# One core, a feed-forward, attention, feed-forward chain: the order of the routing work in the first two blocks

## The reference

```
x = x + 0.5 * ffn(layernorm(x))
x = x + attention(layernorm(x))
x = x + 0.5 * ffn(layernorm(x))

ffn(h):   z = w_norm * h * rsqrt(mean(h*h) + 1e-6)
          probs = softmax(z @ w_router)                      # 32 experts
          w, sel = top_k(probs, 4)
          each expert takes its tokens in order of arrival, 128 at most:
              y_e = (silu(z_e @ w_gate[e]) * (z_e @ w_up[e])) @ w_down[e]    # width 176
          out = sum of w * y_e over the chosen experts
          shared = sigmoid(z @ w_shared_gate) * (silu(z @ sw_gate) * (z @ sw_up)) @ sw_down   # width 704
          return h + out + shared
attention: 16 query heads, 8 key and value heads of width 32, rotary positions,
           scores capped by 50 * tanh(s / 50), causal softmax, output projection
```

## Time and profile before

| | before |
|---|---|
| median of 3 runs | 939.04 us |
| profiled execution | 939.21 us, its span 937.5 us |
| TensorE busy | 910.2 us (97% of the span) |
| VectorE busy | 696.1 us (74%) |
| ScalarE busy | 531.8 us (57%) |
| GpSimd busy | 511.3 us (55%) |
| mean granted TensorE clock | 0.999 |

### The profile page before, as it was taken

One profiled execution on the slowest core, in us unless ns is written; L12 is line 12 of the kernel. 1 busy time (PEld: TensorE's weight loads), 2 busy tenths in 40 slices (PEclk: granted clock), 3 DMA queues, 4 the chain that ended last, 5 costly groups with the idle time before them and its releaser, 6 DMA issues.

```text
span 937.5 us, 18000 instructions
## 1 busy us (share of the span) xinstructions
PE 910.2 (97%) x6118; PEld 685.5 (73%) x6118; DVE 696.1 (74%) x1704; ACT 531.8 (57%) x794; POOL 511.3 (55%) x537
## 2 busy tenths in 40 slices
PE   7999999999999999999999999989999999999997
PEld 6878887777778856666666666558788877777786
DVE  6998787554444889989998999988887875544435
ACT  6666743132233478878887888876667431322322
POOL 6343305555652588887888788934432045655530
PEclk9999999999999999999999999999999999999999
DMA  8143228777774510010001002004432187777725
GB/s 260 49 137 107 74 86 214 178 178 182 181 191 92 179 46 24 23 42 26 23 23 45 22 12 79 24 12 131 142 99 73 56 232 173 183 178 183 173 38 178
DMA packets 95512, 101.89 MB, mean 109 GB/s; under 512 B 18768, under 2 KB 86736, under 8 KB 95440
## 3 DMA queue, kind: packets, MB, share of 16 engines
q1 hardware_dynamic: 83152, 83.17, 28.7%
q0 software_dynamic: 12288, 17.83, 11.2%
HBM read 65.44 MB, written 35.54 MB: 108 GB/s over the span
## 4 chain that ended last, share of the span: by engine, by line
PE 67%; DVE 18%; issue 6%; ACT 5%; POOL 3%; DMA 0%; DVEq 0%; POOLq 0%; SPq 0%; ACTq 0%
PE zT L1048 8%; PE gu L1068 7%; PE gu L90 7%; PE gu L92 6%; PE gu L91 6%; PE pj_at L90 3%; PE down L90 3%; PE down L92 3%; PE down L91 3%; PE pv_at L1766 3%; PE pj_at L92 3%; PE pj_at L91 3%; PE zT L1057 2%; PE scores_at L1750 2%; DVE turned_at L2008 2%
## 5 line engine op out<-in xcount | busy, mean ns | idle before, releaser
L90 PE MATMUL gu<-x_hi,gu_hi 128*128 128x512 f32 x264 | 120.7, 457 | 0.8 <-DVE act_gu L1351 0.7
L820 POOL DMA_INDIRECT rows<-z_rows,slots x64 | 69.0, 1078 | 67.7 <-DVE slots L1342 49.1
L1868 ACT ACTIVATE capped_at<-scores_at 128x2048 f32<-128x2048 f32 x64 | 93.1, 1455 | 20.5 <-PE scores_at L1750 20.2
L92 PE MATMUL gu<-x_lo,gu_hi 128*128 128x512 f32 x264 | 103.9, 394 | 0.0
L91 PE MATMUL gu<-x_hi,gu_lo 128*128 128x512 f32 x264 | 103.6, 392 | 0.0
L1128 ACT CAST a_hi<-act_gu 128x512 fp32r<-128x512 f32 x96 | 59.2, 617 | 75.9 <-DVE act_gu L1351 63.1
L1876 ACT ACTIVATE probs_at<-capped_at 128x2048 f32<-128x2048 f32 x64 | 95.1, 1486 | 2.5
L90 PE MATMUL down<-down_hi,a_hi 128*128 128x256 f32 x300 | 93.9, 313 | 0.6 <-DVE a_lo L1361 0.4
L1230 ACT ACTIVATE y<-gu,rows 128x256 f32<-128x256 f32 x64 | 30.3, 474 | 109.7 <-PE gu L1068 94.6
L1945 POOL TENSOR_SCALAR_AFFINE_SELECT probs_at<-probs_at 128x1024 f32<-128x1024 f32 x64 | 85.6, 1342 | 9.6 <-ACT probs_at L1876 8.9
L1048 PE MATMUL zT<-w_gu,xT 128*128 128x352 f32 x256 | 86.3, 460 | 0.0
(11 more groups left out here) (262 smaller groups left out, 2602.5 us busy)
## 6 DMA issues: line engine op xcount, KB each, us to landing
w_gu<-in_w_gate SPq DMA_DIRECT2D x64, 176.0 KB, 2.6
w_gu<-in_w_up SPq DMA_DIRECT2D x64, 176.0 KB, 3.2
w_down<-in_w_down SPq DMA_DIRECT2D x64, 176.0 KB
z_rows<-z SPq DMA_DIRECT2D x16, 512.0 KB, 3.8
acc<-base SPq DMA_DIRECT2D x10, 512.0 KB, 3.2
out<-base SPq DMA_DIRECT2D x10, 512.0 KB, 3.2
xn_at<-acc SPq DMA_DIRECT2D x16, 256.0 KB, 2.7
x<-xn_at SPq DMA_DIRECT2D x16, 256.0 KB, 2.1
```

The source lines that it names most:

```text
L90: nc.tensor.matmul(out, w_hi, x_hi, start=first, stop=False)
L92: return nc.tensor.matmul(out, w_hi, x_lo, start=False, stop=last)
L820: pool.indirect_dma_start(out=gathered_rows[:, n, :], out_offset=None, in_=m.z_rows, in_offset=bass.IndirectOffsetOnAxis(ap=slots[:, e:e + ...
L1868: nc.scalar.activation(capped[:, u % 2, :, 0:n], scores[:, :, 0:n], ACT.Tanh, scale=QK_SCALE / SOFTCAP).then_inc(capped_ready, 1)
```

## The change

TensorE, for block 0 in `slot`: `router(2)` now stands ahead of `count(1)`, not behind it. For other blocks and in the second stage nothing changes there.

VectorE, block 0 (`first_slot`): `statistics(3)` is written out as its two parts, and `take_counts(1)` stands between them; before, it stood behind `outputs(0, 0)`.

VectorE, block 1 of the first stage (`slot`): `product(1, 3)` stands ahead of `top_experts(3)`, and `weigh(2)` behind `top_experts(3)`; before, `weigh(2)` stood ahead of `a_lo_part(1, 0)` and the product behind the ranking. No instruction is added or taken away.

```diff
@@ on_tensor, slot @@
                 down_block(b)
+                if s is not None:
+                    router(s)
                 if b == 0:
                     count(r)
-                if s is not None:
-                    router(s)
@@ on_vector, first_slot @@
                 weigh(f)
                 top_experts(r)
-                statistics(s + 1)
+                for j in range(TJ):
+                    read = front.read(dve, s + 1, j)
+                take_counts(r)
+                front.variances(dve, s + 1, read)
                 outputs(0, 0)
-                take_counts(r)
                 weigh(r)
                 outputs(0, 1)
@@ on_vector, slot @@
                 product(b, 1)
-                if b == 1 and not before:
+                behind_head = b == 1 and not before
+                if behind_head:
                     statistics(s)
-                weigh(f)
+                else:
+                    weigh(f)
                 a_lo_part(b, 0)
                 a_lo_part(b, 1)
                 product(b, 2)
+                if behind_head:
+                    product(b, 3)
                 top_experts(r)
-                product(b, 3)
+                if behind_head:
+                    weigh(f)
+                else:
+                    product(b, 3)
                 a_lo_part(b, 2)
```

## The result

In 19 runs of each kernel, taken in alternation, the changed kernel has a median of 941.05 us (939.67 to 945.30) against 939.13 (939.01 to 939.55). The ratio on record is 1.0018, with a 95% interval of 1.0012 to 1.0025; the two medians alone give 1.0020. The time lies inside the forecast range of 938.2 to 941.4. Whether the loss is under or over 0.2% is not decided: the ratio is just under it, the interval reaches to both sides, and 941.05 is over the 940.9 us at which the prediction drew that line.

A forecast was written before the change was run, and what follows sets the result against it. TensorE, busy nearly all the time, was taken as the bound. Router and counts -0.05, block 1 to +0.9, handed on to +1.3 us: 939.04 becomes 940.3 us; range for eight in ten 938.2 to 941.4.

The forecast's parts named there:

- Router and counts: Blocks 0 and 1: TensorE's stands of 1.02 and 0.52 us go, but are spent waiting for z(3); worth -0.05 us.
- The copy within the statistics: VectorE, block 0: the counts' copy delays the aggregation of block 3's statistics by 0.05 us, bounds 0 and 0.13.
- Block 1: VectorE stands 2 us before product(1,3); late low parts make TensorE's down projection wait; +0.9 us at its sixth part.
- The gain at chunk 10: TensorE, block 1: the 0.69 us stand ahead of chunk 10 goes, so count(3) comes that much earlier.
- Handed on: Into block 2: z(5) on ScalarE delays the copy of block 4's logits, so TensorE's lateness becomes +1.3 us.
- +1.3: The forecast's total lateness in us, reached at the logits of block 4 and taken as kept to the end.
- rival (d): Block 1, between chunks 1 and 2: the new stand and eight spaced transposes cost clock, 1.6 us; 941.9 us, chance 0.07.
- one stretch of 3.1 us: Evidence against a clock loss: from 9.21 to 12.35 only eight spaced transposes ran, and the next matmul was not slower.
- (c): VectorE's full 1.97 us is handed on through low parts, outputs and block 4's router; 941.0 to 941.2 us, chance 0.12.
- (a): Block 1: low parts are early enough after all, only the 0.69 us gain stays; 938.4 us, chance 0.12.
- (b): All three TensorE stands vanish and z(3) does not hold turn(3); 936.8 us, chance 0.05.

The follow-up runs named there:

- e3: The third edit alone (product(1,3) ahead of top_experts(3), weigh(2) behind it) against the kernel before: median 939.87 us, ratio 1.0005.
- e1: The first two edits alone (router(2) ahead of count(1), counts within the statistics) against the kernel before: median 940.63 us, ratio interval 0.9985 to 1.0021.
- e2: The first edit alone (router(2) ahead of count(1)) against the kernel before: three runs at 939.06 to 939.23 us, seven at 939.62 to 940.29, two at 942.55 and 942.79.
- e5: The changed kernel again, nothing altered, to profile a longer execution; against the kernel before: ratio 1.0025, profiled execution 946.22 us.
- e4: The changed kernel with six additional unused matmuls of 512 columns ahead of turn(3): eleven runs at 939.59 to 940.36 us, one at 945.92.

## Why the prediction held, and where not

**Router and counts.** As forecast: both stands vanish, z(3) holds `turn(3)` at the same time. The copy within the statistics, taken at 0.05 us from bounds of 0 and 0.13, cost 0.00. e3 against the changed kernel confirms that the two edits give TensorE nothing.

**Block 1.** The mechanism was right in each step; some sizes were off. VectorE's stand was 1.90 us (forecast 2). The ranking took 66.00 - 62.77 = 3.23 us and not 3.46, the length read from the earlier trace rows; the difference is in its last instruction, `chosen`, 0.93 us there and 0.69 here. So product(1,4) came at 67.97 and not at 68.22, and the low parts some 0.2 earlier than forecast: the stands ended at 69.31 and 70.09, where 69.5 and 70.3 were forecast. That is why the sixth part moved by 0.62 and not by 0.9.

The gain at chunk 10 was mis-sized too, 0.92 at count(3) where 0.69 was forecast. An idle time in a row counts from the modelled end of the last matmul (0.39 us long), while the next can start 0.23 behind its start, 0.16 before that end; so 0.69 of idle time are 0.85 us of delay, and 0.05 is the offset of the two traces. It changed nothing behind it, since TensorE then stood for the low parts: from 67.18 to 72.31 the first ten groups took 5.13 us against 3.59, 1.54 more (forecast 1.5), although the idle times in the rows, 0.81 and 0.15, add up to 0.96. The logits of block 4 moved by 0.97, not 1.3.

**Handed on.** The sum stopped at those logits. I had seen that VectorE follows with less lateness, and did not price it. In the kernel before, the router of block 5 waited for its low parts; when TensorE is late, that wait is covered. The kernel before, then the changed kernel:

```profile
85.04 0.50 PE L90 MATMUL zT<-x_hi,router_hi 128*128 128x512 f32 x1 [0.16 <-DVE x_lo L677]
```

```profile
85.69 0.51 PE L90 MATMUL zT<-x_hi,router_hi 128*128 128x512 f32 x1
```

The counts of block 4 are 0.97 late (85.45 against 84.48), the next logits 0.64 (90.03 against 89.39), and that stays: the six short runs have a median of 939.72, 0.59 over that of before. The term "+1.3" was mis-sized; it is +0.6, half of the difference lost at the logits of block 4 and half at this router.

**Clock, rival (d).** This is where the judgement failed: the sum put the clock at nothing. The rival had 0.07; by the times and clocks of the runs it happened in 12 of 19, and its price of 1.6 us came out (1.5 between the groups, 1.6 in e1's trace). I had set against it one stretch of 3.1 us at the start of one execution, in which the clock held. What holds in one execution need not hold in the next: the changed kernel does both. And the length of 3.1 us was no bound, since in e2 2.0 us were enough. That the price fits is in part luck. It was taken from the slower transposes at the start of the run, read as a low clock, but the clock rows of the kernel before read 1.00 there (columns as at e1), so that reading is not shown:

```profile
3.60:5.00 1.40, 1.32 (x6) 1.32 (x7) 1.36 (x4) 0.00 (x0) 0.54 (x3) 1.00 0.46 64
8.00:9.30 1.30, 1.21 (x12) 0.97 (x9) 1.07 (x4) 0.28 (x1) 1.14 (x6) 1.00 1.03 412
```

The rule of the Trainium skill, page "TensorE: Matmul & The Clock Gate", section "HAM oscillation — how this bites in real kernels", that pauses between bursts put the array back to its low clock, agrees with e1, e2 and e5, where the clock row reads 0.57 to 0.67 behind the stand. The waits in that section's example are longer than the stand of e2; here the measurement decides. e4 shows the cause: with the stand filled the long group is gone. That the eight transposes have a part in it is not shown; e2 does without them. What decides between the two outcomes in one and the same kernel stays open.

The median of 941.05 lies 0.75 over the forecast, the sum of a constant part forecast 0.7 too large and a clock part left out of it. That it fell inside the range is luck in part. The range held it because it reached over (c), which didn't happen, and because two errors of opposite sign met: with the forecast's +1.3, a long run would be at (d)'s 941.9, outside. The median also depends on how many runs lose the clock, which nobody had priced. The chance for slower by over 0.2% was, by what the runs show, too small: twelve of the 19 runs are 0.16 to 0.30% longer than the median of before, and one 0.66%.

**Rivals (a), (b), (c)** are excluded for the changed kernel by its trace: TensorE stood for low parts, z(3) held, and VectorE's 1.7 us was not handed on whole.

## What to carry to other kernels

Pulling work forward on the busiest engine gathered its waits in front of the next fixed date and won nothing here; before doing so, find the date (here z(3)) and have work ready to put in front of it, as chunk 2 was. Two short stands merged into one longer one (1.70 to 1.85 us here) can cost clock on top, and in some executions only, so look at the spread of the runs and each run's clock and not at one profile. When a call is moved ahead of others, ask what then covers the wait for its inputs: the cover may be the very call that was moved behind it.

## What the runs showed of the hardware

With stands of 1.02 and 0.52 us and 3.2 us of work between them (43.98 to 47.20), the 19 runs of before beside the changed kernel lie within 0.54 us, and its profiled execution reads a clock of 1.00 from 40 to 60 us. With one stand of 1.70 us (e2) or 1.83 to 1.85 us (e1, the changed kernel), most runs are longer at a lower mean clock; the profiles of e1, e2 and e5 show TensorE at the 1.2 GHz level behind the stand for about 2 to 3 us (48.3 to 50.8 in e2, 51.5 to 54.6 in e1). Before the fall TensorE was doing dense matmuls up to the stand. The mean clock of a run moves by only 0.002, so the row of a stretch or the starts of the matmuls (0.42 us apart against 0.23) are what to read.
